# Layer 0 attention: the row maxima are subtracted on GpSimd, and the exponential moves behind the transposes

## The reference

```
scores = einsum('bhqd,bhkd->bhqk', qh, kh) * scale
scores = clip(scores, -CLAMP, CLAMP)
scores = scores * decay[None, None, :, :]
attn = softmax(scores, axis=-1)
out = einsum('bhqk,bhkd->bhqd', attn, vh)
```

## Time and profile before

| | |
|---|---|
| median of 3 runs | 2066.48 us (2064.3 to 2073.12) |
| the profiled execution, its own time | 2070.43 us |
| its span in the profile | 2068.6 us |
| PE busy | 1429.8 us (69%) |
| DVE busy | 1321.1 us (64%) |
| ACT busy | 949.1 us (46%) |
| POOL busy | 301.1 us (15%) |
| mean granted TensorE clock | 0.779 |

### The profile page before, as it was taken

One profiled execution on the slowest core, in us unless ns is written; L12 is line 12 of the kernel. 1 busy time (PEld: TensorE's weight loads), 2 busy tenths in 40 slices (PEclk: granted clock), 3 DMA queues, 4 the chain that ended last, 5 costly groups with the idle time before them and its releaser, 6 DMA issues.

```text
span 2068.6 us, 22478 instructions
## 1 busy us (share of the span) xinstructions
PE 1429.8 (69%) x6385; PEld 659.2 (32%) x6386; DVE 1321.1 (64%) x4032; ACT 949.1 (46%) x2207; POOL 301.1 (15%) x380
## 2 busy tenths in 40 slices
PE   6888787886314441055798998882378999999991
PEld 2254444443101210021235554321222343434430
DVE  3288787886888987739656665654175555546532
ACT  2178776786244444312455655540024444445550
POOL 0010101001200000004740100163015101000005
PEclk9778889898655555555799999875557989799995
DMA  7001010100000000011521222211215110111102
GB/s 259 37 18 45 17 46 16 47 1 7 12 1 0 1 0 1 0 61 44 173 69 56 83 82 79 57 48 27 42 34 182 48 24 32 37 44 51 37 26 59
DMA packets 149889, 98.43 MB, mean 48 GB/s; under 512 B 73312, under 2 KB 134053, under 8 KB 149713
## 3 DMA queue, kind: packets, MB, share of 16 engines
q1 hardware_dynamic: 143623, 84.40, 13.8%
q0 software_dynamic: 6144, 12.60, 2.1%
HBM read 60.83 MB, written 35.73 MB: 47 GB/s over the span
## 4 chain that ended last, share of the span: by engine, by line
PE 46%; DVE 28%; issue 8%; SPq 6%; ACT 5%; DMA 5%; POOL 2%; DVEq 0%; POOLq 0%; ACTq 0%
PE PS L396 38%; PE PS L392 5%; DVE RA L1296 4%; DVE RB L939 4%; DVE RA L1298 4%; SPq L1749 3%; DVE nmx L1138 3%; DVE RB L945 2%; POOL RA L1653 2%; PE PS L632 2%; DMA RA<-xd 2%; DMA RA<-mT 1%; ACT RA L1464 1%; SPq L1760 1%; SPq L1762 1%
## 5 line engine op out<-in xcount | busy, mean ns | idle before, releaser
L396 PE MATMUL PS<-RA 72*128 72x512 bf16 (+2 forms) x1360 | 474.3, 434 | 120.4 <-DVE nmx L1138 46.2
L1138 DVE TENSOR_REDUCE nmx<-PS 128x1 f32<-128x512 f32 x512 | 347.7, 686 | 285.1 <-PE PS L396 282.7
L1506 ACT ACTIVATE RA<-PS 128x512 f32<-128x512 f32 x512 | 303.5, 598 | 214.4 <-PE PS L396 205.6
L396 PEld LDWEIGHTS PS<-RA 72*128 72x128 bf16 (+3 forms) x1360 | 125.7, 105 | 375.5 <-issue 203.0
L392 PE MATMUL PS<-ident,RA 128*128 128x128 f32 x1040 | 171.0, 317 | 97.0 <-ACT RB L1458 48.9
L1464 ACT ACTIVATE RA<-RB,nm 128x512 f32<-128x512 f32 x256 | 170.8, 714 | 85.8 <-POOL nm L1718 85.6
L396 PE MATMUL PS<-RA,Vs 128*32 128x512 f32 x1184 | 191.5, 664 | 3.6 <-ACT RA L1506 1.9
L939 DVE TENSOR_SCALAR RB<-PS 128x1024 f32<-128x1024 f32 x128 | 156.2, 1220 | 53.5 <-PE PS L396 53.5
L392 PEld LDWEIGHTS PS<-ident,RA 128*128 128x128 f32 x1040 | 139.6, 162 | 154.9 <-ACT RB L1458 76.0
L1604 ACT ACTIVATE RA<-RA 128x8 f32<-128x8 f32 x511 | 107.4, 210 | 168.5 <-DVE RA L1296 167.7
L945 DVE CUSTOM_DVE_ANT_0 RB<-RB 128x512 f32<-128x512 f32 x256 | 168.8, 696 | 4.4
(11 more groups left out here) (253 smaller groups left out, 1817.6 us busy)
## 6 DMA issues: line engine op xcount, KB each, us to landing
RA<-scr SPq DMA_DIRECT2D x288, 96.0 KB
xd<-Otok SPq DMA_DIRECT2D x36, 256.0 KB, 4.2
RA<-xd SPq DMA_DIRECT2D x72, 128.0 KB, 2.3
scr<-parts SPq DMA_DIRECT2D x48, 128.0 KB
yd<-RB SPq DMA_DIRECT2D x48, 128.0 KB, 1.8
RB<-in_L_ffn_W SPq DMA_DIRECT2D x24, 256.0 KB
scr<-parts SPq DMA_DIRECT2D x64, 48.0 KB
yd<-RA SPq DMA_DIRECT2D x48, 64.0 KB, 1.5
```

Source lines behind the costliest of these rows:

```text
L396: return e.matmul(o, l, r, start=first, stop=last)
L1138: e.tensor_reduce(nmx[:, g % 3, c:c + 1], bank[(6, 0)[i % 2]], AX.X, ALU.max, negate=True).then_inc(*ROWMAX.up(layer, n, i))
L1506: e.activation(PR[k % 5][:, i, :], bank[(1, 5)[i % 2]], ACT.Exp).then_inc(*EXP.up(layer, k, i))
```

## The change

- Y becomes a ring of four whole matrices (one in RB, three in the part of RA where PR was). DVE waits for the transposes of n - 4 in place of the exponentials of n - 1. The clip and the decays are the same instructions.
- POOL no longer negates; it subtracts the maximum from each 128 x 512 block in place, four instructions per step. Its `part_of` steps come two steps later.
- PE transposes these differences, and ACT evicts each transposed block from PSUM with the exponential, into a ring of eight. The copies of blocks (EVAC), the bias tile `nm` and the exponentials from SBUF are gone.
- The value products of a group are spread over four steps, one kt each (for the last group all in one), from step 4g + 6 on. The side tasks are hung on steps accordingly, and `prep` gets steps 1, 3, 4, 5 and 12 of each batch.
- SP writes the parts out at step 10 of a batch, not 8.

```diff
-    Y = RB[:, 2048:4096].rearrange("p (u j k) -> p u j k", u=2, j=2)
+    Y = [t.rearrange("p (a k) -> p a k", a=4) for t in (RB[:, 2048:4096], RA[:, 12288:14336], RA[:, 14336:16384], RA[:, 16384:18432])]
...
+    TURN0 = 2
+    VALUES0 = {(g, kt): 4 * g + 4 + TURN0 + (kt if g < 15 else 0) for g in range(16) for kt in range(4)}
+    PREP0 = (1, 3, 4, 5, 12)
...
# beside(0)
+            for g in range(16):
+                n = VALUES0[g, 3]
+                todo.setdefault(n, []).append(("out4", g))
+                todo.setdefault(n + 1, []).append(("divide", g))
...
# PE
-                            pe.wait_ge(EXP, 0, k, 3)
-                            turned(bk, [PR[k % 3][:, qt, 128 * kt:128 * kt + 128] for qt in range(4)]).then_inc(*TURN.up(k, kt))
-                            free[bk] = [(EVAC, 0, k, kt)]
-                    for kt in (2 * u, 2 * u + 1):
-                        value(0, k, kt)
+                            pe.wait_ge(LESS, k, 3)
+                            turned(bk, [Y[k % 4][:, qt, 128 * kt:128 * kt + 128] for qt in range(4)]).then_inc(*TURN.up(k, kt))
+                            free[bk] = [(EXP, 0, k, kt)]
+                for (g, kt), at in VALUES0.items():
+                    if at == n:
+                        value(0, g, kt)
...
# DVE
-                        if n:
-                            dve.wait_ge(EXP, 0, n - 1, 2 * u + 1)
+                        if n >= 4:
+                            dve.wait_ge(TURN, n - 4, 3)
...
# ACT
-                            e.copy(PT0[k % 6][:, kt, :], bank[4 + kt % 2]).then_inc(*EVAC.up(0, k, kt))
-                    if n < 64:
-                        if u == 0 and n >= 3:
-                            act.wait_ge(TURN, n - 3, 3)
-                        act.wait_ge(NEGMAX, n, u)
-                        for qt in (2 * u, 2 * u + 1):
-                            e.activation(PR[n % 3][:, qt, :], Y[:, u, qt % 2, :], ACT.Exp, bias=nm[:, n % 4, qt:qt + 1]).then_inc(*EXP.up(0, n, qt))
+                            e.activation(PT0[k % 8][:, kt, :], bank[4 + kt % 2], ACT.Exp).then_inc(*EXP.up(0, k, kt))
...
# POOL
-            for u in range(2):
-                if n >= 4:
-                    pool.wait_ge(EXP, 0, n - 4, 2 * u + 1)
-                pool.wait_ge(CLIP, "decay", n, 2 * u + 1)
-                e.tensor_scalar(nm[:, n % 4, 2 * u:2 * u + 2], mx[:, n % 4, 2 * u:2 * u + 2], -1.0, None, ALU.mult).then_inc(*NEGMAX.up(n, u))
-            if n % 16 in (4, 5, 6, 7) and n < 48:
-                part_of(0, n // 16 + 1, n % 16 - 4)
+            for qt in range(4):
+                pool.wait_ge(CLIP, "decay", n, qt)
+                e.tensor_scalar(Y[n % 4][:, qt, :], Y[n % 4][:, qt, :], mx[:, n % 4, qt:qt + 1], None, ALU.subtract).then_inc(*LESS.up(n, qt))
+            if n % 16 in (6, 7, 8, 9) and n < 48:
+                part_of(0, n // 16 + 1, n % 16 - 6)
...
# SP
-                if n % 16 == 8 and n < 48:
+                if n % 16 == (8 if layer else 10) and n < 48:
```

More of the change, by code:

```diff
@@ L233, in build @@
     ones = R[0:1, :]
-    PT0 = [RB[:, 4096 + 2048 * i:4096 + 2048 * i + 2048].rearrange("p (a k) -> p a k", a=4) for i in range(4)] + PR[3:5]
+    PT0 = ([RB[:, 4096 + 2048 * i:4096 + 2048 * i + 2048].rearrange("p (a k) -> p a k", a=4) for i in range(4)] + PR[3:5]
+           + [RA[:, 8192 + 2048 * i:8192 + 2048 * i + 2048].rearrange("p (a k) -> p a k", a=4) for i in range(2)])
     X_IN, CONST, W0, DECAY, ONES, ZERO = loads("x"), loads("const"), loads("w0"), loads("decay"), loads("ones"), loads("zero")
@@ L256, in build @@
     FF_V, GATE_V, SCAN, CARRY, ROUTE, GATED, YO_V, COMB = (signal("dve_" + n) for n in ("ff", "gate", "scan", "carry", "route", "gated", "yo", "comb"))
-    SQ, XT_A, EXP, EVAC, MISC_A, FF_A, GATE_A, TANH, ROUTE_A = (signal("act_" + n) for n in ("sqrt", "xt", "exp", "evac", "misc", "ff", "gate", "tanh", "route"))
+    SQ, XT_A, EXP, MISC_A, FF_A, GATE_A, TANH, ROUTE_A = (signal("act_" + n) for n in ("sqrt", "xt", "exp", "misc", "ff", "gate", "tanh", "route"))
     STEP_H, XG_A, HT_A = signal("act_step"), signal("act_xg"), signal("act_ht")
-    SET, PARTS_P, BIAS_P, NEGMAX = signal("pool_set"), signal("pool_parts"), signal("pool_bias"), signal("pool_negmax")
+    SET, PARTS_P, BIAS_P, LESS = signal("pool_set"), signal("pool_parts"), signal("pool_bias"), signal("pool_less")
+    TURN0 = 2
+    VALUES0 = {(g, kt): 4 * g + 4 + TURN0 + (kt if g < 15 else 0) for g in range(16) for kt in range(4)}
+    PREP0 = (1, 3, 4, 5, 12)
     def beside(layer):
-        lag = 2 if layer == 0 else 6
+        lag = 6
         todo = {}
+        if layer == 0:
+            for g in range(16):
+                n = VALUES0[g, 3]
+                todo.setdefault(n, []).append(("out4", g))
+                todo.setdefault(n + 1, []).append(("divide", g))
+                if g % 4 == 3:
+                    for i, name in enumerate(("otok", "proj", "add")):
+                        todo.setdefault(n + 2 + i, []).append((name, g // 4))
+            for b in range(1, 4):
+                for i, n in enumerate(PREP0):
+                    todo.setdefault(16 * (b - 1) + n, []).append(("prep", b, i))
+            return todo
         for g in range(16):
@@ L276, in beside @@
                     todo.setdefault(n + 2 + i, []).append((name, g // 4))
[L277 to L280, removed]
+        for g in range(16):
+            todo.setdefault(4 * g + 3, []).append(("max", g))
+            todo.setdefault(4 * g + 4, []).append(("maxrow", g))
         for b in range(1, 4):
@@ L283, in beside @@
                 n = 16 * (b - 1) + 1 + i
-                if layer and i == prep_steps[layer] - 1:
+                if i == prep_steps[layer] - 1:
                     n = 16 * (b - 1) + 1 + lag
@@ L513, in value @@
         def value(layer, k, kt):
-            if k < 4 or k % 4 or k > 64:
+            if layer and (k < 4 or k % 4 or k > 64):
                 return
-            g, bk = k // 4 - 1, 6 if layer == 0 else 7
+            g, bk = (k // 4 - 1, 7) if layer else (k, 6)
             if kt == 0:
@@ L521, in value @@
                     pe.wait_ge(MISC_A, "v", layer, g // 4)
-                pe.wait_ge(EVAC if layer == 0 else EXP, layer, k - 1, 3)
+                pe.wait_ge(EXP, layer, 4 * g + 3, 3)
             for j in range(4):
@@ L525, in value @@
                 ins = mm(bank[bk][32 * j:32 * j + 32, :], Vs[:, g // 4 % 2, kt, 9 * (n % 16):9 * (n % 16) + 32],
-                         (PR[n % 5] if layer else PT0[n % 6])[:, kt, :], kt == 0, kt == 3)
+                         (PR[n % 5] if layer else PT0[n % 8])[:, kt, :], kt == 0, kt == 3)
             if kt == 3:
@@ L531, in attention0 @@
         def attention0():
-            for n in range(64 + 8):
-                s, h, k = (n // 4) % 4, n % 4, n - 2
+            for n in range(64 + 10):
+                s, h, k = (n // 4) % 4, n % 4, n - TURN0
                 for u in range(2):
@@ L931, in attention0 @@
             dve.wait_ge(DECAY, "all")
-            for n in range(64 + 8):
-                nb = n % 4
+            for n in range(64 + 10):
                 for u in range(2):
                     if n < 64:
-                        if n:
-                            dve.wait_ge(EXP, 0, n - 1, 2 * u + 1)
+                        if n >= 4:
+                            dve.wait_ge(TURN, n - 4, 3)
                         dve.wait_ge(SCORE, 0, n, u)
-                        e.tensor_scalar(Y[:, u, :, :], PS[:, 2 * u:2 * u + 2, :], C0, -C0, ALU.min, ALU.max).then_inc(*CLIP.up("clip", n, u))
+                        e.tensor_scalar(Y[n % 4][:, 2 * u:2 * u + 2, :], PS[:, 2 * u:2 * u + 2, :], C0, -C0, ALU.min, ALU.max).then_inc(*CLIP.up("clip", n, u))
                         dve.wait_ge(CLIP, "clip", n, u)
-                        if n >= 4:
[L942 to L946, removed]
+                        for qt in (2 * u, 2 * u + 1):
+                            ins = e.tensor_tensor_reduce(out=Y[n % 4][:, qt, :], in0=Y[n % 4][:, qt, :], in1=Dk[:, qt, :], scale=1.0, scalar=NEG,
+                                                         op0=ALU.mult, op1=ALU.max, accum_out=mx[:, n % 4, qt:qt + 1])
                             ins.then_inc(*CLIP.up("decay", n, qt))
@@ L1449, in attention0 @@
         def attention0():
-            for n in range(64 + 8):
-                k = n - 2
+            for n in range(64 + 10):
+                k = n - TURN0
                 for u in range(2):
                     if 0 <= k < 64:
-                        if u == 0 and k >= 6:
-                            act.wait_ge(VALUE, 0, (k - 6) // 4)
+                        if k % 8 == 6:
+                            act.wait_ge(FF_P, "down", 3)
+                        if k >= 8:
+                            act.wait_ge(VALUE, 0, k // 4 - 2)
                         for kt in (2 * u, 2 * u + 1):
                             act.wait_ge(TURN, k, kt)
```

(8 more changed lines are left out.)

3 lines of the change are left out of this document (removed).

## The result

The change makes the kernel slower: 2160.98 us against 2067.99 us of the kernel before beside it (4 runs each), a ratio of 1.0441 with a 95% interval of 1.0396 to 1.0485. That is outside the range of the prediction (2008 to 2110), on the side to which it gave 0.25.

A forecast was written before the change was run, and what follows sets the result against it. DVE was taken as the floor of layer 0 attention, with PE's order and ACT's work 63 us above it. 2070.4 - 51 + 3 + 12 = 2034, for the median 2030 us, 1.8% faster; 8-in-10 range 2008 to 2110.

The forecast's parts named there:

- What bounds the kernel: Layer 0 attention, 397.3 us: DVE is the floor, busy 334.4; PE's order and ACT's eight instructions per step add 63 us.
- ACT: Layer 0 attention: 256 exponentials from PSUM at 0.6 us, 153 us against 305 busy; no gain in itself.
- Of the 62.9 us idle I take 51 back: PE's new order in layer 0 attention: scores are ready before DVE asks, 51 us saved, bounds 30 and 63.
- Rival C: PE becomes the bound in layer 0 attention: clock at 0.75, PE 363 us, total about 2048; chance 0.08.
- C's sign: TensorE's granted clock below 0.87, where the forecast expected it above.
- What one costs, no row shows ... The bounds are 0.60 and 1.17. I take 0.64.: GpSimd's subtraction on 128 x 512: 0.64 us estimated at CAST's rate; two against 1.26 us cost 3 us in all.
- The port: DVE decays and GpSimd's SBUF reads exclude each other by a lock; the clip, which reads PSUM, does not count.
- the window of 1.26 us: Both subtractions of a half run from the next clip's start, with 1.26 us before the next decay wants the lock.
- Rival A: GpSimd's subtraction takes 1.17 us, so each half's first decay waits 1.08 us longer: 138 us, total 2156; chance 0.16.
- The splits: POOL's three batches of splits, 19 us of lock, find the clip's window filled: at most 17 us more, 12 taken.
- Rings and SP: Rings of 4 and 8, and SP's later writing of the parts: no cost, unless POOL is late.
- The prediction's own range of 2012 to 2050: The forecast's own range for the whole kernel: 63 or 30 us idle recovered, splits 0 to 17, subtraction 0.60 to 0.68.

## Why the prediction was wrong

- *What bounds the kernel.* Right. DVE is the floor at 334 us, and the 63 us above it were PE's order and ACT's work: without the subtraction DVE's wait before the clip is 0.0.
- *ACT.* Right: 256 at 0.596 us, forecast 0.6; the stage's ACT time is 159 us, forecast near 170.
- *PE, "Of the 62.9 us idle I take 51 back".* Right in mechanism, 58.5 measured. Rival C was wrong: with DVE as the bound the clock was granted at 0.97, not less. In the changed kernel itself it fell to 0.81, which the prediction had named as C's sign; but PE was busy only 343 of 491 us there and waited for POOL, and with the subtraction left out the clock was back: a consequence and not a cause.
- *The step that failed: "What one costs, no row shows ... The bounds are 0.60 and 1.17. I take 0.64."* An undisturbed subtraction takes 1.556 us, above both ends. From the earlier trace rows, 0.215 us for 2 columns, it is 2.6 ns a column, where CAST has 0.84. The nearest rows were of other operations, and the row of the same operation, at two columns, holds nothing of its rate. The Trainium skill ("GPSIMD Engine Reference", Engine selection) puts one-input operations at roughly line rate; CAST at 0.84 ns a column agrees, TENSOR_SCALAR with a per-row scalar or a constant does not (1.56 and 1.48 us for 512). The Trainium skill's figure for a tight loop (same page, Elementwise — side-by-side cycle accounting), 769 ns for 512 elements, is half of what is measured.
- *The step that was missing.* The prediction priced a subtraction only by what it keeps from DVE at the port, and left out that GpSimd is itself a queue: four in a step must take less than 4.97 us, 1.24 us each. No rival had GpSimd's own throughput as the bound. It is what set the stage's length: POOL is busy 489 of 491 us, and even with the port taken away 406 of 408.
- *The port.* Right that decays and subtractions exclude each other, in both directions, and right in the window of 1.26 us: at one TENSOR_TENSOR a half next to nothing is lost, at two of them the next decay waits 0.58 us. This is the exclusive lock of the Trainium skill ("SBUF — State Buffer", Who interferes with whom), and the runs that let the decays read PSUM agree: they give back 74 and 76 us. Wrong was who pays. The prediction had DVE wait; in the change GpSimd waits, 0.31 us a subtraction, and being the bound, it pays nearly all.
- *Rival A* gave 2156 us and 2161 was measured, which is chance. It had decays of 1.2 us on average; they are 0.72, so the waits it counted as 138 us were 8. Where its mechanism did act (TENSOR_TENSOR, decays 0.98), it cost 75 us, 0.58 us a half. Its rule, two subtractions less the clip's 1.26 us, gives 0.80 a half with the 1.03 us measured: it asks over a third too much.
- *The splits,* 12 us: on POOL they are 19 us of the bound.
- *Rings and SP:* nothing, as forecast; in no run did PE wait for a stack.
- *Slips in the sums.* The prediction's own range of 2012 to 2050 is narrower than the bounds it names. Those give 2066.5 - 63 = 2004 at one end and 2066.5 - 30 + 17 + 13 = 2066 at the other. Rival C's 363 us is set 17 above 346, the stage without the 3 and 12 us of POOL; above the forecast's own stage of 361 it is 2. Neither would have brought 2161 into reach.

## What to carry to other kernels

Before an elementwise operation goes to GpSimd, price it from a row of the same operation at the same size, and check it twice: its sum against the period of the engine that sets the pace, and its place between the DVE instructions that read two SBUF inputs. Here one instruction of 1.03 us per half fits under a clip from PSUM and is nearly free, two cost 0.58 us a half, and 1.56 us ones overrun the period by themselves. And when a change bundles a reordering with a move to another engine, run them apart: the reordering was worth 1.6% alone, and the whole with half of the subtractions on ScalarE and the others as TENSOR_TENSOR 2.6 to 2.8%, where the bundle lost 4%.

## What the runs showed of the hardware that was not expected

- On GpSimd, subtracting a per-row value from 128 x 512 float32 takes 1.556 us as TENSOR_SCALAR, 1.48 with a constant, and 1.03 as TENSOR_TENSOR with the value broadcast, although the latter has two tensor inputs. A TENSOR_TENSOR on two full tensors took 1.17, on 18 x 512 and with bfloat16 output, so this comparison is a rough one.
- Which engine gives way at the shared port depended on the form: with the scalar from memory GpSimd was stretched by 0.31 us on average and decays by 0.03; with a constant GpSimd by 0.09 and decays by 0.23; as TENSOR_TENSOR both, GpSimd by 0.20 and decays by 0.29. A subtraction with the scalar from memory that started inside the first decay of a half let the second decay, which was issued after it, go first, 78 of 79 times. The constant form is one run. The cause stays open.
- The granted clock of TensorE rose from 0.87 to 0.97 in a stage in which PE did the same work in 59 us less, and was 0.91 where the value products came in one row of 16 instead.
